# Three graph stages on one core: lanes as streams over all graphs in place of passes, and matmuls without a use in most waits of TensorE

## The reference, cut to what matters

```python
def kernel(x, adj, ...):                  # x (16, 512, 128), adj (16, 512, 512)
    G0: 3 steps of a gated graph network (messages = adj @ h, then a GRU cell)
    F0: mixture of 8 experts of width 256, two chosen per node
    G1: graph attention, one head          F1: attention over 64 slices, 8 heads
    G2: mean over neighbours, two products F2: a Mamba-2 block, chunks of 128, 4 heads
    G3: masked attention, 4 heads, twice   F3: router that keeps half of the nodes, MLP of width 512
    return x
```

## Time and profile before

| | |
|---|---|
| median of 3 runs | 3164.19 us (3164.08 to 3169.1) |
| the profiled execution | 3173.81 us, span 3172.0 us |
| TensorE busy | 2954.1 us, 93% |
| DVE busy | 2200.5 us, 69% |
| ScalarE busy | 1671.8 us, 53% |
| POOL busy | 656.2 us, 21% |
| mean granted TensorE clock | 0.969 |
| stores of graph 0 and of graph 15 issued at | 414.4 us and 3169.3 us |

### The profile page before, as it was taken

How to read it: one execution, slowest core, us unless ns; L and a number is a source line. 1 busy time by engine, 2 the same in 40 slices (tenths; PEclk the granted TensorE clock), 3 DMA queues, 4 the chain that set the end, 5 groups by cost and what they waited for, 6 DMA issues and landing times.

```text
span 3172.0 us, 54106 instructions
## 1 busy us (share of the span) xinstructions
PE 2954.1 (93%) x20355; PEld 1997.8 (63%) x20386; DVE 2200.5 (69%) x7047; ACT 1671.8 (53%) x3346; POOL 656.2 (21%) x788
## 2 busy tenths in 40 slices
PE   7879999999999999999999999999999999999888
PEld 3556665666666666665666666566666666666665
DVE  3457777767777776777777677777767777676654
ACT  1426556554664646456564655645465465546534
POOL 0011313112131221213122130312213031121302
PEclk8989999999999999999999999999999999999999
DMA  3000000000000000000000000000000000000000
GB/s 125 17 4 18 1 24 1 24 1 8 18 1 24 1 12 13 4 21 1 24 1 11 14 5 21 1 24 1 8 18 1 24 1 8 1 4 4 2 8 5
DMA packets 28740, 40.13 MB, mean 13 GB/s; under 512 B 1344, under 2 KB 17728, under 8 KB 28224
## 3 DMA queue, kind: packets, MB, share of 16 engines
q1 hardware_dynamic: 28480, 36.67, 3.6%
HBM read 28.28 MB, written 4.19 MB: 10 GB/s over the span
## 4 chain that ended last, share of the span: by engine, by line
PE 78%; DVE 11%; ACT 8%; issue 2%; POOL 1%; DMA 1%; another core or an unknown queue 0%; SPq 0%; DVEq 0%; ACTq 0%
PE ps L439 65%; PE ps L917 6%; ACT scratch L1079 5%; DVE scratch L1397 2%; ACT L1079 2%; PE ps L446 2%; DVE scratch L1400 1%; DVE x L1403 1%; DVE scratch L1899 1%; PE ps L617 1%; PE ps L583 1%; DVE scratch L1916 1%; PE ps L803 1%; DVE stats L1413 1%; PE ps L765 1%
## 5 line engine op out<-in xcount | busy, mean ns | idle before, releaser
L1079 ACT ACTIVATE scratch<-scratch 128x512 f32<-128x512 f32 (+4 forms) x832 | 568.0, 695 | 152.5 <-DVE scratch L1899 95.0
L439 PE MATMUL ps<-scratch 128*128 128x128 f32 (+6 forms) x4608 | 539.4, 380 | 31.9 <-DVE scratch L1397 17.0
L439 PEld LDWEIGHTS ps<-weights_sb,scratch 128*128 128x128 f32 (+3 forms) x3840 | 447.3, 182 | 155.5 <-issue 121.0
L2130 POOL TENSOR_SCALAR scratch<-scratch 128x512 f32<-128x512 f32 x512 | 359.5, 719 | 742.4 <-DVE scratch L1906 741.8
L439 PE MATMUL ps<-weights_sb,scratch 128*128 128x128 f32 (+3 forms) x3840 | 495.4, 278 | 3.2 <-DVE x L1403 1.8
L439 PE MATMUL ps<-xT,weights_sb 128*128 128x512 f32 x864 | 474.6, 648 | 12.1 <-ACT xT L1079 11.0
L1079 ACT ACTIVATE scratch<-ps,weights_sb 128x512 f32<-128x512 f32 x368 | 252.2, 686 | 378.9 <-PE ps L439 378.3
L439 PEld LDWEIGHTS ps<-scratch 128*128 128x128 f32 (+5 forms) x4608 | 335.5, 160 | 179.4 <-issue 74.7
L1899 DVE CUSTOM_DVE_ANT_0 scratch<-ps,nomask 128x512 f32<-128x512 f32 x512 | 335.1, 684 | 29.5 <-PE ps L439 28.9
L917 PEld LDWEIGHTS ps<-weights_sb,scratch 128*128 128x128 f32 x2048 | 228.6, 140 | 195.5 <-issue 115.6
L917 PE MATMUL ps<-weights_sb,scratch 128*128 128x128 f32 x2048 | 305.2, 277 | 21.7 <-ACT adjf L1079 8.7
(11 more groups left out here) (174 smaller groups left out, 4584.3 us busy)
## 6 DMA issues: line engine op xcount, KB each, us to landing
adj<-adj SPq DMA_DIRECT2D x16, 1024.0 KB, 5.4
weights_sb<-weights SPq DMA_DIRECT2D x1, 4605.0 KB, 22.7
x_in<-x SPq DMA_DIRECT2D x16, 256.0 KB, 2.8
scratch<-scratch SPq DMA_DIRECT2D x32, 128.0 KB, 2.3
out<-x SPq DMA_DIRECT2D x16, 256.0 KB, 2.3
scratch<-raw SPq DMA_DIRECT2D x1, 1645.0 KB, 12.3
weights_sb<-weights SPq DMA_DIRECT2D x1, 499.0 KB, 6.8
scratch<-raw SPq DMA_DIRECT2D x1, 384.0 KB, 4.1
```

The source lines that it names most:

```text
L439: return pe.matmul(o, lhsT, rhs, start=start, stop=stop, **k)
L1079: return act.activation(o, a, func, **k)
L2130: pool.tensor_scalar(p, p, cut(g, G3_RI + n, 1), 1.0, ALU.mult, ALU.mult).then_inc(s["att_p"], 1)
```

## The change

The three lanes become generators that run over all 16 graphs without end points (`lane_of`), and `lanes_run` takes the place of `thirds`: 17 loops over the tables, no lane is run to its end before the last. The loops' strings are cut at other places: the second loop holds one graph more in lanes a and e and the first graph of lane l, and 13 loops use the third string. All five tables are new. In PE_TURNS the digits go from 48, 67, 21, 120 and 305 (the third string used 14 times) to 187, 359, 72, 263 and 413 (the third used 13 times): 834 calls of `keep_bank` become 2158, 1668 matmuls become 4316. In `prepare` on TensorE each of the eight triplets of small products is a turn of its own. Two waits are added on ScalarE ahead of a graph's adjacency copy, and one on DVE ahead of the layer normalisation of F0, which the ends of the passes had made needless.

```diff
 PE_TURNS = (
-    ("ppaaaaaaaaaaaa1111111111111111aaaaaaaaaaa7777777777777777aaaaaaaaaaa7777777777777777a"),
...
+    ("7777777ppppp777777ap111ap1111aaaa111111aappa111111aa111111111111111111a666666a6666666aaaa666666aa7777777a77777"
...
-        def phase(stages, g):
-
-            for stage in stages:
-                yield from stage(g)
-
-        def thirds(turns, stages, prepare=None, keep_bank=None):
-
-            for h in range(graphs + 2):
-                run = {lane: phase(stages[n], h - n) if 0 <= h - n < graphs else iter(()) for n, lane in enumerate("ael")}
-                run["p"] = prepare() if prepare and not h else iter(())
-                for turn in turns[min(h, 2) if h < graphs else h - graphs + 3]:
+        def lane_of(stages):
+
+            for g in range(graphs):
+                for stage in stages:
+                    yield from stage(g)
+
+        def lanes_run(turns, stages, prepare=None, keep_bank=None):
+
+            run = {lane: lane_of(stages[n]) for n, lane in enumerate("ael")}
+            run["p"] = prepare() if prepare else iter(())
+            for lane in run:
+                next(run[lane], None)
+            for h in range(graphs + 1):
+                for turn in turns[min(h, 2) if h < graphs - 1 else h - graphs + 4]:
                     if turn.isdigit():
                         keep_bank(int(turn))
                     else:
                         next(run[turn], None)
-                for which in "pael":
-                    for _ in run[which]:
-                        pass
+            for which in "pael":
+                for _ in run[which]:
+                    pass
...
                     for h in range(SH):
+                        yield
                         pe.matmul(lp(1, SG, P, h * SG), R("f1_wxT", SD)[:, tile(h)], R("f1_wslice", SD), start=True, stop=True)
...
                     for t in range(T):
                         yield
+                        if t == 0:
+                            act.wait_ge(*done("x_first", g))
+                            if g >= LANES:
+                                act.wait_ge(*done("pv_psum", g - LANES, 3))
                         last = f(AF[g][:, t, :], ADJ[g][:, t, :], ACT.Copy)
...
                     v.wait_ge(*x_done(g, n - 1))
+                    if n == F0 and g >= LANES:
+                        v.wait_ge(*x_done(g - LANES, F3))
                     for t in range(T):
                         last = v.bn_stats(stats[g][:, t, :], src[:, t, 0:D])
```

More of the change, by code:

```diff
@@ L78 @@
 SP_TURNS = (
[L79 to L83, removed]
+    ("eala"),
+    ("el"),
+    ("lael"),
+    ("lelal"),
+    ("l"),
 )
 PE_TURNS = (
-    ("ppaaaaaaaaaaaa1111111111111111aaaaaaaaaaa7777777777777777aaaaaaaaaaa7777777777777777a"),
-    ("aeaeeeeaeeaaaeaeeeeeeeeeeeeeeeeeeaeeeeeeeeeeeeaeeeeeeeeeeeeeaeeeeeaa77777777777777777aeeeeaeeeaaaaaeaeeeaeeeea"
-     "a777777777777777777777777777777777777eaeeeeaeaaeeeaaeeeeeeaaeeeeeaeeeeeeaa77777777777777eeeeeeeeeea"),
@@ L96 @@
[L96 to L99, removed]
+    ("7777777ppppp777777ap111ap1111aaaa111111aappa111111aa111111111111111111a666666a6666666aaaa666666aa7777777a77777"
+     "7aa777777777777777777a777777a7777777aaaa777777aa7777777a777777aa777777777777777777a777777777777777777777777777"
+     "777eeee7777777e"),
@@ L100 @@
 )
 ACT_TURNS = (
[L102 to L108, removed]
+    ("aaaaapaaaaaaaaaaeeeeeeeeea"),
@@ new lines @@
+    ("eeeaeeeeeeeaeeaeaeaeeeeaeeeeeeeeeeaeaaeaeaeeeeeeeeaeeeeeaaellllllllallealllleeeelllllllleaeeeeeeleaeeeleaeeele"
+     "aelllallllllelelellleaeleleeeeeeleelelllallallleleallllalllellellllleelleelelaelllllleleeleeaalllelelllll"),
+    ("llllalallllleeellllllllaeeeeeeeeeleeeaeeleealeeelllllallallleleelllleeaeeleeeeleeelellaallllllelelallleallllle"
+     "llelellleelellellalllellaeeleealllelelllll"),
+    ("llllleeleelellleelllllllleeeeeeleeeeeleeleelllllllllleleellleleleeeeeleeelellellllllelelllllllelellellllelelee"
+     "lelllllllelleeeellleelllllllllllll"),
@@ new lines @@
+    ("laellealleeeeellllleelaaaeaaeeallllllllllalllllelleaeleeellellleeleeeeellaellealellallelellealllleealelllleele"
+     "ellelllllllaeeleelellaealllllllllaeeeeeeeaaelllllelleelllllleelelleleellelelelaeelelellllleeelellealealeeaeell"
+     "elllalaeeeel"),
+    ("leallleleeeeellllleeleeeeelllllelellellelllleleeelellleleellllllelleelllelllellelllleelelllleeelelllelllllleel"
+     "lleeelelllllllleleeeeeeellllllleellllleellleleleeeelllleleeeelelllllleelleelleleeeeellelllleeeelellellleeeeell"
+     "ll"),
@@ L119 @@
     ("llllllllllllllllllllllllllllllllllllllllllllllllllllllllllllllllllllllllllllllllllllllllllllllllllllllllllllll"
-     "lllllllllll"),
+     "llllllll"),
 )
 POOL_TURNS = (
[L123 to L127, removed]
+    ("aeaeeee"),
+    ("eeeelealllllllellllllllllllleellllllelelleelllllllle"),
+    ("llalelllllllellllllllllllellelllelleleellllllllle"),
@@ L128 @@
+    ("llelllllllelllllllllllllellllelellleeelll"),
+    ("llllllellllllllllllllllllllllllllllllllllllllll"),
 )
```

51 lines of the change are left out of this document (31 added, 20 removed).

## The result

| | before | with the change |
|---|---|---|
| median | 3165.4 us (3164.1 to 3169.1, 4 runs) | 3148.9 us (3147.7 to 3150.6, 4 runs) |
| ratio | | 0.9941, interval 0.9926 to 0.9956 |
| the profiled execution | 3173.8 us, span 3172.0 | 3149.1 us, span 3147.3 |

A forecast was written before the change was run, and what follows sets the result against it. TensorE was taken to set the period, its idle time and low clock being winnable. Terms 42 + 9 + 8 + 6 = 65 us took the profiled 3173.8 to 3109, then 0.3% lower to 3099 us; range 3071 to 3140.

The forecast's parts named there:

- the last step: Whole run: from the profiled execution's 3109 us to a median 0.3% lower, 3099 us.
- B: Rival: clock stays up, but new waits of about 2 us a period pay part back; 3127 us, chance 0.15.
- a period of 183 to 184.5: Full periods between F2's transposes: length in us that would show the prediction right, against 186.8 before.
- The price of a low stretch: TensorE at half clock behind F2's transposes: loses 3.1 us (long) or 1.6 (short), mean 2.3 us a period.
- Edit 2, the order: New turn tables in the full periods: 0.7 us less each; with clock held up, 3.0 in each of 14, 42 us.
- Edit 1, fills: 2648 more fill matmuls, 148 us of TensorE time, lie in its idle waits and cost nothing; bounds 0 and 148.
- Rival E: Fills outlast their waits, all 148 us on the path: 83 us slower, 3247 us, chance 0.05.
- Edit 3, the preparation: Preparation cut up at the start: first stage about 6 us earlier, clock lifted sooner for 3 us; together 9 us.
- Edit 4: More fills in the two filling and two draining windows: 8 us from filling, 6 us from drain.
- Edit 5: Streams in place of passes, and three new waits on ScalarE and DVE: 0 us.
- D: Rival: low-clock dips stay in full periods, only the start and some windows gain 18 us; 3146 us, chance 0.05.
- C: Rival: every microsecond at low clock returns half, 98 us, plus 10 for waits and 6 for start; 3050, chance 0.07.

The follow-up runs named there:

- The delay that is free behind the seam and dear in the experts: Changed kernel plus 14 digits (28 fill matmuls): behind the second 512-column product after F2's transposes, 3150.4 us; amid F0's experts, 3170.2 us.
- the kernel with the old order: Changed kernel's streams, waits, filling and draining orders, but the 14 full passes in the previous kernel's order with 39 and 6 fill digits at F2's transposes: 3135.4 us.
- The first experiment: Kernel before, order untouched, with 39 fill digits ahead of the four F2 transposes and 6 behind in each of 14 full passes: 3143.3 us, ratio 0.993.
- the warm start: Kernel with old-order full passes and the change's ends, plus 56 matmuls on ones before the first loads and 30 behind the first preparation products: 3136.7 us.

## Why the prediction was wrong

The profiled execution was to become 3109 and became 3149: 40 us of the 65 are missing. Another 10 stem from the last step, below. The sign that the forecast gave for B came true, the clock up and the period above 185; its sign of a period of 183 to 184.5 did not.

**The price of a low stretch** is the step that failed first. "Both meet at 184.5: this is what the old order would give with the clock held up." The kernel before with the seam's fills gives 185.2. The two checks agreed because each took off, from the measured period, what three products had lost at half clock, as if TensorE's time counted there. The same trace says otherwise, in rows that were not read. F2's states on TensorE, before, behind the seams at 417.31 and 604.80:

```profile
447.24 1.16 PE L439 MATMUL ps<-scratch 128*128 128x128 f32 x8 [0.30 <-DVE scratch L1397]
```

```profile
633.78 1.16 PE L439 MATMUL ps<-scratch 128*128 128x128 f32 x8 [0.29 <-DVE scratch L1397]
```

They begin 29.93 us behind the seam after a long dip, 28.98 after a short one, and 28.0 after none (the kernel before with the seam's fills), each time when DVE's result arrives. The long dip moves them by 1.9 us, not 3.1, the short one by 1.0, not 1.6. The delay that is free behind the seam and dear in the experts shows why. Missing: 0.7 us in each of 14 periods, 10 us.

On this the Trainium skill, TensorE: Matmul & The Clock Gate, section Terms, goes further off: half of every low microsecond. The 14 low stretches at the seams of the full passes average 8.5 us (seven of 10.2, seven of 6.8), which makes 4.2 us, an estimate by the page's rule; the runs show 1.6 in the old order and, with stretches of 8.1 us on the mean, 0.9 in the new.

**Edit 2, the order** was to give 0.7 us a period and costs 0.74 (185.94 - 185.2): 13 x 1.44 = 19 us missing. The text looked at how much TensorE would stand, and took the sequence as "nearly the old one". What decides is three DVE steps, of 0.38 to 0.42 us each, ahead of F2's convolution. The step that the text did name, the first stage's statistics that moved up into the rank steps, did no harm: putting them back was not tried, but the period went down to 185.10 with them where they are. The first full period was counted as one like the others and is 5.7 us over 185.2 instead of 0.7 under: 6 us missing. It stands in the second string, whose second half no row was read for. The kernel with the old strings has 185.29 there, so it is the strings; whether it is their order or their 86 further fill matmuls (4.8 us of TensorE) stays open. The chain of waits runs through fills for 3.4 us of this period and for 1.6 us of a later one, where taking the small ones out changed nothing.

**Edit 1, fills at nothing**: right. The seam's wait of 4.8 us holds 78 of them with 0.49 us left bare, and with the small ones taken out the period is the same. That is shown for thirteen of the full periods. The fills of the filling and draining windows and of the first full period were not taken out by themselves, so for them it is not shown. Rival E, a kernel 83 us slower, is refuted.

**Edit 3, the preparation**: 9 forecast, 6.1 measured, within its bounds of 3 and 12. The first transposes were 5.2 us earlier (24.69 against 29.90), about as forecast, and of the 3 us from an earlier clock 0.9 came. This number moves from one execution to the next: the first x leaves stage one at 76.0 to 82.5 us in the kernels that share the change's start.

**Edit 4**: filling 5.4 of 8 (bounds 0 and 11), drain 6.35 of 6, both against the profiled execution before. How much of that is the fills' doing is another matter, as the last step shows. **Edit 5**, streams and waits at 0: right, since the kernel with the old order has both and the period of before with its seam filled.

**The last step.** The forecast took 9.6 us off because the profiled execution before was that much above its median. After, the two are equal (3149.1 and 3148.9). One reason stands in the trace of before, in a window that the argument had no row for:

```profile
193.30:210.40 17.10, 15.46 (x81) 0.50 0.00 0
```

It belongs to that execution and not to the kernel. The first experiment's kernel issues the same instructions up to the last transposes ahead of the first seam, and its execution has no such stretch (3.4 us at half clock is all that it records there). At 194 us the two are 0.5 us apart. Behind the stretch the same transposes on TensorE stand at, before and in that kernel:

```profile
224.10 0.60 PE L507 MATMUL ps<-weights_sb,xT_first 128*128 128x128 f32 x4
```

```profile
217.35 0.60 PE L507 MATMUL ps<-weights_sb,xT_first 128*128 128x128 f32 x4
```

That is 6.75 us without any edit, and the first seam keeps them (230.77 against 224.02). The draining windows, whose strings are the same too, are 182.48 and 139.76 us there in place of 183.00 and 143.38. Together that is 10.9 us, and the 9.6 need no other cause (the other execution was itself 1.6 us under its median); the forecast took much of them off twice, as edits and as the distance to the median. Read against that execution, the change's start, filling and drain give 4.7, 0.1 and 2.2 us where 9, 8 and 6 were forecast. It is one execution of each, so these three numbers are as uncertain as the difference between the two.

Added up, in profiled executions: 10 (price) + 19 (order) + 6 (first period) + 3 (start) + 2.6 (filling) - 0.35 (drain) = 40 us, and 10 from the last step: 3099 becomes 3149.

**The rivals.** B, "the new order pays part of it back", had the right mechanism and nearly the right size for a period, 1 us of gain where 0.85 was measured; it named DVE, but as the way into F2's normalised rows, where the cost lies behind them. That its size fits is in part luck: it took 2 us for the new order off a gain of 3.0, and the runs show 0.74 for the order and 1.6 for the dips. Its 0.15 was too little: the order had the widest bounds of all terms, and its best value had been taken from a count of idle time. D fell, since no dip is left in a full period. C fell, with 3050 against 3148.9.

## To carry to other kernels

Before time at a seam is given a price, ask what paces the stretch behind it: two kernels with the same 1.6 us of fill, one behind the seam and one in the middle, cost 0.11 and 1.60 us a period, and that one pair would have told that the price of the dip lay below what the slow products lost. When an order changes on all queues, compare the start of the longest dependent chain against the period's own mark, here the first step of the convolution on DVE, rather than the sums of idle time; the largest bare wait can be a symptom that moves to the next instruction when its releaser is made early. And run a large change's smallest part alone first: 45 digits in one string beat the whole of it, and the old order with the new ends beats both. Before a window of one execution is made the ground of a term, look at the same window in a second execution of the same instructions: here the filling differed by 6.75 us.

## What the runs showed of the hardware

Small products did not keep TensorE's clock up. Timeline of TensorE in the kernel with the warm start, the same step of the first and the second triplet:

```profile
15.47 0.43 PE L1074 MATMUL ps<-scratch 64*128 64x64 f32 x2
...
16.53 0.69 PE L1074 MATMUL ps<-scratch 64*128 64x64 f32 x2
```

The clock fell between the two, at the head of a stretch of 17.1 us in which TensorE was busy for all of it. Fill matmuls of 128 columns in bf16, 78 in 4.5 us, did keep it up at every seam between the full periods of the change; with them taken out the dips are back. With the warm start a dip of 3.4 us stands behind the first seam in spite of them. Why it fell at the start, whether by the products' size or by something else of that stretch, was not tested.

The granted clock of the records is not always there. The page after gives 1.00 for the first 80 us, but a product of 512 columns (two records) at 27.95 takes twice what one takes later:

```profile
27.95 2.02 PE L455 MATMUL ps<-xT_first,weights_sb 128*128 128x512 f32 x2
...
59.51 1.02 PE L455 MATMUL ps<-scratch_first,made_sb 128*128 128x512 f32 x2
```

In the kernel with the old order such a product takes 2.02 us too, at 26.68, inside a recorded stretch at 0.50. So TensorE ran at 1.2 GHz there in the change as well, as in eight of the eleven other kernels with the change's streams, whose records have a low stretch of 13.7 to 20.5 us from 13.4 to 16.2 us on. The first 56 matmuls of the warm start are such a case too, 0.10 us each where those of the earlier trace rows take 0.056, with no low stretch on record:

```profile
1.04 5.64 PE L285 MATMUL ps<-ones_bf 128*128 128x128 bf16 x56 [1.04 <-DVE ones_bf L296]
```

The duration of a known product is the better witness.
